# Cross-attention and a routed feed-forward on one core: four equal parts of 16 batches, gate products three gathers behind, two rows in a descriptor

## The reference

```python
x = x + xattn(layernorm(x), ctx_768, ...)            # q,k,v, softmax, w_out, b_out
x2 = layernorm(x).reshape(-1, H)                     # H = 128
logits = x2 @ router_w.T
_, idx = top_k(softmax(logits), 2)
gate[t, idx] += logits[t, idx]
for e in range(8):                                   # I = 176
    moe += gate[:, e:e+1] * ((silu(x2 @ w1[e].T) * (x2 @ w3[e].T)) @ w2[e].T)
moe += (silu(x2 @ sw1.T) * (x2 @ sw3.T)) @ sw2.T     # the shared expert
x = x + moe
```

## Time and profile before

| | |
|---|---|
| median of 3 executions | 1026.05 us (1024.22 to 1027.2) |
| the profiled execution | 1016.84 us |
| its span, first to last instruction | 1014.8 us |
| its mean granted TensorE clock | 0.972 |
| busy share PE, DVE, ACT, POOL | 93%, 80%, 63%, 73% |

### The profile page before, as it was taken

The page is one execution under the profiler, slowest core; times in us unless marked ns, Lnnn a source line. Parts: engine busy times, 40 slices in busy tenths (PEclk is TensorE's granted clock), DMA queues, the critical chain, the costliest instruction groups (busy, mean ns, idle before and its releaser), DMA issues. The chain is left out here.

```text
span 1014.8 us, 29059 instructions
## 1 busy us (share of the span) xinstructions
PE 941.7 (93%) x9838; PEld 792.7 (78%) x9838; DVE 816.5 (80%) x1912; ACT 634.7 (63%) x1354; POOL 745.7 (73%) x1107
## 2 busy tenths in 40 slices
PE   7999999999999999999999999996988889999970
PEld 6688878888887888888788888865887769987750
DVE  4899999999999999999999999995654346555772
ACT  4677778977777777777787877764333234444320
POOL 5356565787888788888878878887655850888885
PEclk9999999999999999999999999999999889999995
DMA  9224254333443433332434333254455454569542
GB/s 275 52 44 95 63 121 132 59 82 79 103 93 82 64 71 76 65 81 59 84 88 95 67 67 78 62 126 114 135 178 146 131 152 126 165 161 178 128 148 75
DMA packets 224894, 106.55 MB, mean 105 GB/s; under 512 B 160705, under 2 KB 215521, under 8 KB 224001
## 3 DMA queue, kind: packets, MB, share of 16 engines
q1 hardware_dynamic: 216560, 87.91, 37.1%
q0 software_dynamic: 8192, 16.79, 6.2%
HBM read 38.59 MB, written 34.60 MB: 72 GB/s over the span
## 5 line engine op out<-in xcount | busy, mean ns | idle before, releaser
L558 POOL TENSOR_TENSOR O_lo<-O,O_hi 128x512 f16<-128x512 f32 x128 | 146.5, 1164 | 91.7 <-ACT O_hi L738 91.7
L1064 DVE TENSOR_TENSOR pt_lo<-Q,pt_hi 77x512 f16<-77x512 f32 x256 | 163.8, 680 | 11.9 <-ACT pt_hi L730 10.6
L624 POOL DMA_INDIRECT ctx_raw<-ys,pos_y x128 | 127.4, 995 | 61.4 <-DMA ys<-ysb 35.1
L508 POOL DMA_INDIRECT xs<-x2cat,pos x128 | 131.6, 1028 | 45.7 <-issue 43.1
L730 ACT ACTIVATE pt_hi<-Q 77x512 f16<-77x512 f32 x256 | 139.2, 589 | 15.7 <-PE Q L1329 5.2
L1329 PE MATMUL Q<-ident,P 128*77 128x128 f32 x1024 | 139.9, 278 | 6.7 <-DVE pt_lo L1064 5.8
L1259 PE MATMUL S<-G,xTm 128*128 128x462 f32 (+1 forms) x384 | 145.5, 514 | 0.0
L706 ACT ACTIVATE v_hi<-W,sc 77x512 f16<-77x512 f32 x128 | 87.7, 687 | 91.2 <-PE W L1189 90.7
L1329 PEld LDWEIGHTS Q<-ident,P 128*77 128x77 f32 x1024 | 111.7, 148 | 10.0 <-issue 8.7
L1259 PEld LDWEIGHTS S<-G,xTm 128*128 128x128 f32 x384 | 67.0, 191 | 53.3 <-issue 36.8
L1023 DVE TENSOR_REDUCE top<-S 128x6 f32<-128x462 f32 (+1 forms) x192 | 104.8, 572 | 0.5 <-PE S L1259 0.4
(11 more groups left out here) (270 smaller groups left out, 2880.3 us busy)
## 6 DMA issues: line engine op xcount, KB each, us to landing
ys<-ysb SPq DMA_DIRECT2D x44, 256.0 KB
xg_early<-xs SPq DMA_DIRECT2D x60, 128.0 KB
xp<-x2cat SPq DMA_DIRECT2D x64, 64.0 KB, 1.7
y_out<-X SPq DMA_DIRECT2D x16, 256.0 KB
xg_late<-xs SPq DMA_DIRECT2D x28, 128.0 KB
xs<-zero_in SPq DMA_DIRECT2D x24, 128.0 KB, 2.5
X<-x_in SPq DMA_DIRECT2D x9, 256.0 KB, 2.7
xs<-x2cat,pos POOLq DMA_INDIRECT x128, 2.5
```

The source lines that it names most:

```text
L508: pool.indirect_dma_start(out=xs_d[batch_part(b)][:, :], out_offset=index(pos, b, k), in_=x2cat[:, b % RING, :], in_offset=None).then_inc( ...
L558: pool.tensor_tensor(O_lo[:, half_], O[:, (t + 1) % 2, half_], O_hi[:, half_], ALU.subtract).then_inc(s["p_Olo"], 1)
L624: pool.indirect_dma_start(out=Yr[:, u % YR, i * D:(i + 1) * D], out_offset=None, in_=ys_d[batch_part(b)][:, :], in_offset=index(pos_y, b, ...
L1064: dve.tensor_tensor(pt_lo[0:NK, j % 2, c * 512:(c + 1) * 512], QB[q_bank(j, c)][0:NK, :], pt_hi[0:NK, j % 2, c * 512:(c + 1) * 512], ALU.s ...
```

## The change

Three things change.

1. **Parts.** `PART` becomes 16, 16, 16, 16. Every part has 24 granules and 12 routed steps, so there are 96 granules and 48 routed steps in place of 88 and 44. There is a fourth `xs`, `ys` and table; the 12 pieces of the parts' tables lie in the slots 27 to 50, 51 to 70, 71 to 82 and 83 to 94, and the zeros of the third and fourth part in the iterations 16 to 19 and 28 to 31. The outputs that a part's first gather waits for are 0 to 11, 12 to 23, 24 to 35 and 36 to 47; before they were 0 to 11, 12 to 27 and 28 to 43. `add_at` follows: 22, 24, 25, 27, 29, 30, 32, 34, 35, 37, 39, 40, 42, 44, 45, 47, 49, 50, 52, 53, 55, 57, 58, 60, 62, 63, 65, 67, 68, 70, 72, 73. PE's last iteration is 65, the last `shared_add` is in 66.
2. **Gates.** POOL's loop runs over single gathers g = 0 to 127. Each has a semaphore of a ring of 8. The gate product of tile g stands behind gather g + 3 and waits for the landing of gather g; gather g also waits for the landing of gather g - 8. DVE's last 8 units wait for each tile.
3. **Descriptors.** The rows of a granule go to partitions in pairs: partition p takes rows 2p and 2p + 1 in place of p and p + 128, in the load of `xs` and in the store of `ys` alike. Two neighbouring rows are 1024 bytes in one piece.

```diff
-PART = [16, 24, 24]
+PART = [16, 16, 16, 16]
...
-        def gathered(eng, u):
-            wait(eng, f"ga{u % YR}", 16 * GB * (u // YR + 1))
+        def landed(eng, g):
+            wait(eng, f"ga{g % GR}", 16 * (g // GR + 1))
...
-                                     xs_d[p][ds(v, GRAN), :].rearrange("(i p) n -> p i n", p=128)).then_inc(ring, 16)
+                                     xs_d[p][ds(v, GRAN), :].rearrange("(p i) n -> p i n", i=2)).then_inc(ring, 16)
...
-                sp.dma_start(ys_d[p][first:first + NT, :].rearrange("(i p) n -> p i n", p=128),
-                             ysb[:, m % 3, :].rearrange("p (i n) -> p i n", n=D)).then_inc(s[f"st_y{m % 3}"], 16)
+                sp.dma_start(ys_d[p][first:first + NT, :].rearrange("(q p i) n -> p q i n", p=128, i=2),
+                             ysb[:, m % 3, :].rearrange("p (q i n) -> p q i n", i=2, n=D)).then_inc(s[f"st_y{m % 3}"], 16)
...
+            def gather(g):
+                u, i = g // GB, g % GB
...
+                    wait(pool, "e_add", u - YR + 1)
+                if g >= AHEAD:
+                    landed(pool, g - AHEAD)
...
+            def gate_row(g):
+                u, i = g // GB, g % GB
+                b, k = u // 2 * GB + i, u % 2
+                landed(pool, g)
...
-            GATE_AGE = 2
-            for u in range(2 * NS + GATE_AGE):
...
+            GATE_AGE = 3
+            for g in range(2 * NB):
+                gather(g)
+                if on(g - GATE_AGE, 0, GATED * GB):
+                    gate_row(g - GATE_AGE)
...
-                    gathered(dve, u)
                     dve.wait_ge(s["d_gate"], q * GB // CB + 1)
                     for i in range(GB):
+                        landed(dve, u * GB + i)
```

More of the change, by code:

```diff
@@ L164, in program @@
         w2_raw = sb("w2_raw", [128, 2 * WE])
-        YR = 8
+        YR, GR = 8, 8
         xg_early = sb("xg_early", [128, XG_EARLY, GB * 2 * D], HF)
@@ L198, in program @@
         names = ("ld_x0 ld_x1 ld_x2 ld_x3 ld_ctx0 ld_ctx1 ld_ctx2 ld_qk0 ld_qk1 ld_wv ld_wo ld_w1 ld_w3 ld_id "
-                 "ld_w2e ld_w2 ld_kc ld_hc zs zx0 zx1 zx2 st_out "
+                 "ld_w2e ld_w2 ld_kc ld_hc zs zx0 zx1 zx2 zx3 st_out "
                  "amax_zero amax_done amax_all m_turn m_low m_wide m_pow scale_step wv_lo_done "
@@ L209, in program @@
                  "xg0 xg1 xg2 xg3 xg4 xg5 st_y0 st_y1 st_y2").split()
-        names += [f"sc{k}_{r}" for k in range(2) for r in range(SCR)] + [f"xp{r}" for r in range(4)] + [f"ga{r}" for r in range(YR)]
+        names += [f"sc{k}_{r}" for k in range(2) for r in range(SCR)] + [f"xp{r}" for r in range(4)] + [f"ga{r}" for r in range(GR)]
         s = {n: sem(n) for n in names}
@@ L314, in program @@
         GATED = 24
+        AHEAD = GR
         add_at, free = [], 0.0
@@ L621, in _ @@
             pool.wait_ge(s["s_O"], 3 * NB)
-            def gather(u, i):
-                b, k = u // 2 * GB + i, u % 2
-                pool.indirect_dma_start(out=Yr[:, u % YR, i * D:(i + 1) * D], out_offset=None, in_=ys_d[batch_part(b)][:, :],
-                                        in_offset=index(pos_y, b, k)).then_inc(s[f"ga{u % YR}"], 16)
-            def gate_row(u, i):
+            def gather(g):
+                u, i = g // GB, g % GB
                 b, k = u // 2 * GB + i, u % 2
                 if i == 0:
-                    gathered(pool, u)
+                    p = batch_part(b)
+                    if b == sum(PART[:p]) and k == 0:
+                        for r in range(3):
+                            pool.wait_ge(s[f"st_y{r}"], 16 * len(range(r, first_of(p + 1), 3)))
+                        pool.wait_ge(s["d_posy"], p + 1)
+                    wait(pool, "e_add", u - YR + 1)
+                if g >= AHEAD:
+                    landed(pool, g - AHEAD)
+                pool.indirect_dma_start(out=Yr[:, u % YR, i * D:(i + 1) * D], out_offset=None, in_=ys_d[batch_part(b)][:, :],
+                                        in_offset=index(pos_y, b, k)).then_inc(s[f"ga{g % GR}"], 16)
+            def gate_row(g):
+                u, i = g // GB, g % GB
+                b, k = u // 2 * GB + i, u % 2
+                landed(pool, g)
+                if i == 0:
                     pool.wait_ge(s["d_gate"], b // CB + 1)
@@ L639, in _ @@
             pool.wait_ge(s["w2_done"], 1)
-            GATE_AGE = 2
-            for u in range(2 * NS + GATE_AGE):
-                if u < 2 * NS:
-                    p = batch_part(u // 2 * GB)
-                    if u // 2 * GB == sum(PART[:p]) and u % 2 == 0:
-                        for r in range(3):
-                            pool.wait_ge(s[f"st_y{r}"], 16 * len(range(r, first_of(p + 1), 3)))
-                        pool.wait_ge(s["d_posy"], p + 1)
-                    wait(pool, "e_add", u - YR + 1)
-                    if 0 < u < GATE_AGE:
-                        gathered(pool, u - 1)
-                for i in range(GB):
-                    if u < 2 * NS:
-                        gather(u, i)
-                    if 0 <= u - GATE_AGE < GATED:
-                        gate_row(u - GATE_AGE, i)
+            GATE_AGE = 3
[3 more added lines that the diff above has]
+                    gate_row(g - GATE_AGE)
         @block.scalar
```

## The result

On the chip of the first comparison the changed kernel was slower:

| | before | changed |
|---|---|---|
| median (lowest to highest), us | 1025.26 (1024.22 to 1027.2), 4 runs | 1046.62 (1041.74 to 1047.45), 4 runs |
| profiled execution, us | 1016.84, span 1014.8 | 1046.97, span 1045.1 |
| ratio, with 95% interval | | 1.020 (1.0165 to 1.0235) |

A forecast was written before the change was run, and what follows sets the result against it. POOL's gathers were taken to bound the end, then PE's chain: 999.75 + 0.75 + 6.17 + 2.48 = 1009.15 us of span for 1014.8, 5.65 gained. With 9.2 us from profiled execution (1011.2) to median: 1020.4 us, range 1010 to 1030.

The forecast's parts named there:

- The mechanism of the gain: End of the program: earlier gathers take POOL off the path, PE's chain sets the end; 5.65 us gained, chance 0.54.
- last shared add: Last add that needs PE: four more routed steps at 4.20 us move its start 16.8 us, from 982.95 to 999.75.
- the five units: DVE's units 27 to 31, still to be added behind the last shared add: 1.233 us each, 6.17 us together.
- The descriptors: Loads and stores in 1024-byte pieces: worth 0 to 0.8 us, taken as 0, since PE's own work covers them.
- the price of PE's steps after the change: Routed steps after the change: 4.20 us each, as beside gathers they took 4.26; shared iterations 3.45 us as before.
- gathers, table pieces and zeros at once: Outputs 12 to 20, steps of 6.71 us: a second such stretch of five steps was feared after the change.
- Rival A: Five steps from output 24: slow steps come back, 2.5 us more each, 12.5 us, deciding from 1.75 a step; chance 0.16.
- The gate scheme: Gate product three gathers behind its gather on POOL: cost 0, and the old 1.82 us wait it removes worth nothing.
- Waits of POOL for landings: POOL's gate products: 5.7 us from gather start to product against landings near 2.8 us, so no waiting, cost 0.
- Tables and zeros: Fourth part's table pieces on DVE and zero transfers on SP: cost 0, from above 7.5 us.
- the loads four steps ahead: SP's loads: together with the ring of three outputs they cover the delay by added zeros, cost 0.
- the 9.2 us between the profiled execution and the median: Whole kernel: the median shown lies 9.2 us above the profiled execution, kept for the changed kernel, 1011.2 to 1020.4.

The follow-up runs named there:

- e5: The changed kernel unedited, run again: 984.94 us, 0.993 of the kernel before.
- e3: The kernel before with the two-row (1024-byte) pieces alone, old parts and gate scheme: 991.68 us, 0.999 of the kernel before.
- e10: The kernel before without the indirect gathers of y, their buffers zeroed once: 976.13 us, 0.960 of the kernel before.
- e18: The changed kernel without gate products on POOL and with DVE's unit adds earlier (pace 1.35, age 3): 1132.64 us, 1.103 of the kernel before.
- e9: The changed kernel with DVE's adds of gathered units two iterations earlier (age 3 for 5): 1031.78 us, 1.016 of the kernel before.
- e2: The kernel before with the new gate scheme alone, old parts and one-row pieces: 988.69 us, 0.995 of the kernel before.
- e13: The changed kernel unedited, run again in another set: 986.43 us, 0.994 of the kernel before.
- e16: The changed kernel without gate products on POOL and with earlier unit adds (pace 1.35, age 3): 983.01 us, 0.991 of the kernel before.

## Why the prediction was wrong

**The mechanism of the gain was right, where steps keep 4.20 us.** In even sets the changed kernel gains 6.9 and 6.3 us (ratios 0.993 and 0.994), for a forecast of 5.65. By steps: POOL leaves the end (last gather at 970.67, last shared add at 973.79, in e5), the five units cost 6.04 us for 6.17. The last shared add moved by 17.5 us for 16.8, and there luck helped: the four steps and the late loads at two part starts cost 19.2, and e5's second stage began 1.7 us earlier. The descriptors were worth 0 (e3).

**The step that failed is the price of PE's steps after the change.** I took 4.20 us for the routed steps and the old distances for the shared ones, because steps 27 to 43 took 4.26 beside gathers. Those were gathers with a product between, one every 1.62 us. The 23 ungated gathers of the earlier trace rows, one every 1.27 us, ran in the kernel before when PE had finished. The change moves the ungated ones up beside the shared steps. I worked that out (949.6 to 989.9) and gave it no price on PE; the text asked only whether POOL would be late. The stretch of the shared steps became 16.6 us longer in the first comparison, the largest of the three pieces; the same steps beside gated gathers stood 3.73 us apart in the kernel before. For this place I had no row: the only ungated gathers beside PE in the kernel before are the first eight, from 777.93 us, and there the steps were slow. I named that stretch, "gathers, table pieces and zeros at once", and did not see that its gathers began without products. That gathers beside PE are the cause of slow steps in an uneven set is shown by e10, which has none of either, and by e18; that the ungated ones among them cost these 16.6 us is read from where the gaps lie. No run took them, or one of the three edits, out of the changed kernel in an uneven set.

**Rival A came true, and explains 9.5 of the 36.2 us.** From output 24 (853.46) to 29 (883.94) five steps took 30.5 us instead of 21.0, 9.5 us, or 1.9 us a step, over its threshold of 1.75. I had given it 0.16 and said that steps 27 to 43 spoke against it. Its cause was named too narrowly: "gathers, table pieces and zeros at once". e18 shows that gathers alone suffice at a high rate. Why the gated gathers of part 1 cost 7.3 of 50 us in the changed kernel and those of the kernel before 1 of 116 stays open; zeros beside them may add to it, and no run took the zeros away, but e9, with the same zeros and pieces there, lacks only 2.2 of 49.

**Until output 20** the changed kernel lost 7.9 us beside the first part's gathers. The kernel before has nearly the same work there, and no run ties this piece to the change: outputs 12 to 20 took 53.7 us in the kernel before, 59.9 in the changed one, and 50.0 in e9, which differs from the changed one only in the place of DVE's adds. The larger part of this piece lies beside gathers with products, 12.7 of 43 us that PE lacks from 786 us on.

**The gate scheme** was costed at 0 and is worth 3.7 us by medians where POOL is last (e2), 2.1 us by the spans of e2 and e3. I had counted the five products fewer in the fourth part, but not as a gain of its own, and overlooked the landing signal of the last unit. Waits of POOL for landings stayed free, as forecast.

**Tables and zeros** were costed at 0. In even sets the steps of e5 beside pieces and zeros keep 4.20 us but for one of 4.47, but the loads four steps ahead do not cover all: the first load of the third and the fourth part comes late behind its zeros, and beside gathers the steps there take 1.2 us more each, 2.4 us together (e5).

**The baseline was treated as the kernel's own.** The 6.71 us of steps 12 to 20 belong to an uneven set: in e3 they take 4.22 us on average. So, it seems, do the 9.2 us between the profiled execution and the median: e3's profiled execution is 0.1 us from its median, and e13's 1.5. They were carried over to the changed kernel, whose profiled execution is 0.35 us above its median. So the median missed by 26.2 us where the span missed by 35.95: this term hid 9.6 us of the miss by luck. The kernel before loses 25 to 33 us in an uneven set; the 25.2 us of its profiled span against e3's go one path: output 27 is copied at 859.56 instead of 834.73 (e3), and POOL's chain to the end starts with it.

## What to carry to other kernels

A change that takes an engine off the end of the program puts its work beside another engine's, and the price there has to be read from a row in which both run at the same density, not from the nearest row in which both run. Slow steps without a releaser ("issue" or "remote" on several engines at once) are a warning: find out what else runs in exactly those windows before using steps from another stretch, and take the work away once (here: no gathers) to see whether it is the cause. Where such steps exist, compare in more than one set and on more than one chip: one kernel was 1% faster than before in one set (e16) and 10% slower in another (e18).

## What the runs showed of the hardware

- Indirect gathers of 128 rows of 512 bytes, issued by GpSimd every 1.25 us, can bring the other engines of the core nearly to a halt in some sets: PE busy 9.24 of 40 us, DVE 1.34, SP without a transfer for 34 us (e18), though part of what DVE, ACT and SP lack is their wait for PE. The same program in another set shows PE busy 35.85 of 37 us (e16). With a product between, one every 1.57 to 1.61 us, the loss went from 6.9 of 44 us to 0.1 of 52 (e9).
- During the halt DMA engines are idle about three quarters of the time (share 0.21 to 0.30 in e18). The Trainium skill, page "SBUF — State Buffer", section "Who interferes with whom", says that DMA never contends with a compute engine, and that a DMA can be starved by DVE through GpSimd's descriptor writing. The runs show a case in the other direction: POOL's gathers keep their pace and the compute engines stop. SP's MOVE, a register instruction, takes up to 0.71 us there beside the loads (e18) and 0.04 in an even set (e16), so it is not the engines that work on data alone. Whether a memory port, the delivery of instructions or something else outside the core stops them, no run here shows.
- The condition holds through a set (seven and nine runs of the kernel before, within 5 us) and changed between sets on one chip (11).
